# Transposes of activations by DMA instead of by TensorE, in an attention and FP4 FFN layer on eight cores

## The reference

```python
xn = layernorm(x)
q, k, v = xn @ WQ, xn @ WK, xn @ WV            # 16 heads of 64
attn = softmax(causal(q @ k.T / 8)) @ v @ WO
xq = fp4_quant_dequant(xn)                     # blocks of 16 along the last dim
h = silu(xq @ fp4(w_gate).T) * (xq @ fp4(w_up).T)      # 2816 wide
out = x + attn + fp4_quant_dequant(h) @ fp4(w_down).T
```

## Time and profile before

| | us |
|---|---|
| median of the runs | 8919.08 (8908.66 to 8929.5, 2 runs) |
| profiled execution, its own time | 8984.06 |
| its span, slowest core (core 5) | 8982.5 |
| spans of the eight cores | 8902.6 to 8982.5 |
| mean granted TensorE clock, dies 0 and 1 | 0.771 and 0.761 |

### The profile page before, as it was taken

The page is one execution under the profiler, slowest core; times in us unless marked ns, Lnnn a source line. Parts: engine busy times, 40 slices in busy tenths (PEclk is TensorE's granted clock), DMA queues, the critical chain, the costliest instruction groups (busy, mean ns, idle before and its releaser), DMA issues.

```text
span 8982.5 us, 81694 instructions; the slowest of 8 cores (8902.6 to 8982.5 us)
## 1 busy us (share of the span) xinstructions
PE 5393.8 (60%) x21392; PEld 2186.3 (24%) x21392; DVE 3172.4 (35%) x5268; ACT 2391.1 (27%) x4112; POOL 2267.7 (25%) x2237
## 2 busy tenths in 40 slices
PE   0000147665788457665778457666778367656877
PEld 0000013111333222111333222112333122112333
DVE  2444460001566540000666530001666530002665
ACT  0000133551111234550111234550111325541111
POOL 1434330110334221120333211110334211110443
PEclk9999968666888667666888676667888676667887
DMA  4222200002100100002110100002000100011000
GB/s 127 56 57 68 68 24 10 1 1 88 67 36 36 54 17 10 1 1 103 54 40 36 50 24 1 1 26 107 29 36 36 54 19 1 1 63 71 36 36 36
DMA packets 137330, 354.95 MB, mean 40 GB/s; under 512 B 76352, under 2 KB 77376, under 8 KB 132160
## 3 DMA queue, kind: packets, MB, share of 16 engines
q1 hardware_dynamic: 136896, 349.74, 11.2%
HBM read 255.85 MB, written 93.85 MB: 39 GB/s over the span
## 4 chain that ended last, share of the span: by engine, by line
PE 38%; DVE 25%; issue 10%; ACT 10%; DMA 8%; POOL 6%; DVEq 1%; SPq 1%; POOLq 0%; ACTq 0%
PE ps_c L610 10%; DVE heap L235 5%; ACT heap L597 4%; DVE heap L226 4%; POOL heap L604 4%; DVE heap L257 3%; PE ps_a L790 3%; PE ps_a L582 3%; DVE heap L229 3%; PE ps_a L548 3%; PE ps_b L548 3%; PE ps_c L697 3%; PE ps_a L732 2%; DVE heap L238 2%; DVE heap L810 2%
## 5 line engine op out<-in xcount | busy, mean ns | idle before, releaser
L245 POOL TENSOR_TENSOR heap<-heap 128x512 f32<-128x512 f32 (+3 forms) x564 | 914.0, 1621 | 3976.1 <-DVE heap L241 3976.1
L610 PE MATMUL ps_c<-heap 128*65 128x512 bf16 (+3 forms) x2560 | 1092.6, 463 | 766.7 <-POOL heap L604 372.6
L623 DVE CAST heap<-ps_c 64x512 bf16<-64x512 f32 x256 | 174.9, 683 | 2713.6 <-PE ps_c L610 2674.8
L604 POOL TENSOR_TENSOR heap<-heap,tri 128x128 bf16<-128x128 bf16 x1024 | 435.2, 425 | 2448.2 <-ACT heap L597 2336.9
L597 ACT ACTIVATE heap<-ps_a 128x512 bf16<-128x512 f32 (+1 forms) x1280 | 639.9, 551 | 728.0 <-PE ps_a L582 712.7
L247 POOL TENSOR_TENSOR heap<-heap 128x512 f32<-128x512 f32 (+3 forms) x564 | 764.5, 1355 | 81.7 <-POOL heap L245 1.3
L610 PEld LDWEIGHTS ps_c<-heap 128*65 128x65 bf16 x2560 | 312.9, 122 | 1654.3 <-issue 1641.7
L840 PE MATMUL ps_c<-heap 128*128 128x512 bf16 x2816 | 682.5, 407 | 5.0 <-ACT heap L874 5.0
L226 DVE TENSOR_REDUCE heap<-heap 128x32 f32<-128x512 f32 (+3 forms) x564 | 412.5, 731 | 504.4 <-DMA heap<-w_up 167.1
L597 ACT ACTIVATE heap<-ps_b 128x512 bf16<-128x512 f32 (+2 forms) x1280 | 590.6, 524 | 0.0
L235 DVE TENSOR_TENSOR heap<-heap 128x512 f32<-128x512 f32 (+3 forms) x564 | 501.2, 889 | 60.9 <-DVE heap L232 2.8
(11 more groups left out here) (78 smaller groups left out, 6302.7 us busy)
## 6 DMA issues: line engine op xcount, KB each, us to landing
heap<-x SPq DMA_DIRECT2D x128, 512.0 KB, 3.3
attn_scr<-heap SPq DMA_DIRECT2D x64, 512.0 KB, 2.6
heap<-attn_scr SPq DMA_DIRECT2D x64, 512.0 KB
out<-heap SPq DMA_DIRECT2D x64, 512.0 KB, 2.6
heap<-wg_d SPq DMA_DIRECT2D x4, 5632.0 KB, 19.8
heap<-wu_d SPq DMA_DIRECT2D x4, 5632.0 KB, 34.1
heap<-wd_d SPq DMA_DIRECT2D x4, 5632.0 KB
heap<-w_gate SPq DMA_DIRECT2D x22, 512.0 KB, 4.1
```

The lines of the kernel that those rows point to most:

```text
L245: P.emit("gpsimd", lambda e: e.tensor_tensor(u, u, M, op=ALU.add), waits=[(s_ve, ve_m), (s_po, s_po.n)], inc=(s_po, 1))
L604: P.emit("gpsimd", lambda e, eb=eb: e.tensor_tensor(eb[:, 0:128], eb[:, 0:128], tri[:], op=ALU.mult), waits=[(s_ac, ac_exp), (s_po, s_po.n ...
L610: pr=pr, s_=s_, vst=vst, jm=jmax: e.matmul(pv[:, off:off + n], vst[:, j, pr * 2 + s_, 0:65], eb[:, 0:n], start=(j == 0), stop=(j == jm - 1)),
```

## The change

The 128x128 transposes of xnb, xnq and hq are taken off TensorE, and their copies off ACT. In their place SP issues dma_start_transpose, one for each 128x128 block, from SBUF straight to the block's place in xnt, xnqt and hqt in SBUF. The weights' transposes in the first stage stay on TensorE. There are three new semaphores, s_trb, s_trq and s_trh, one for each kind. Who waited for TensorE's transpose (to overwrite xnb, xnq or hq) or for ACT's copy (to read xnt, xnqt or hqt) now waits for the DMA's semaphore. The transposes of xnq are no longer one tile late: they follow those of xnb in the same tile.

```diff
 # layer-norm stage, tile t
-                if t >= 1:
-                    pxnq, pt = pending_xnq
-                    for c in range(NCD):
-                        P.emit("tensor", lambda e, pxnq=pxnq, c=c: e.transpose(
...
                 for c in range(NCD):
-                    P.emit("tensor", lambda e, xnb=xnb, c=c: e.transpose(
-                        ps_t[:, c * 128:(c + 1) * 128], xnb[:, c * 128:(c + 1) * 128], idn[:]),
...
+                    P.emit("sync", lambda e, xnb=xnb, c=c, t=t, xnt=xnt: e.dma_start_transpose(
+                        xnt[:, c, t * 128:(t + 1) * 128], xnb[:, c * 128:(c + 1) * 128]),
+                        waits=([(s_ac, ac_xnb), (s_trb, s_trb.n)] if c == 0 else []),
+                        inc=(s_trb, 16))
+                tr_xnb_t = s_trb.n
+                xnb_rd = tr_xnb_t
+                for c in range(NCD):
+                    P.emit("sync", lambda e, xnq=xnq, c=c, t=t, xnqt=xnqt: e.dma_start_transpose(
+                        xnqt[:, c, t * 128:(t + 1) * 128], xnq[:, c * 128:(c + 1) * 128]),
+                        waits=([(s_ve, ve_xnq), (s_trq, s_trq.n)] if c == 0 else []),
+                        inc=(s_trq, 16))
+                xnq_rd[pp] = s_trq.n
+                ac_xnqt.append(s_trq.n)
 # V projection, then Q and K projection: what the first matmul waits for
-                            waits=([(s_ac, ac_xnt_t), (s_w, w_attn_ld)]
+                            waits=([(s_trb, tr_xnb_t), (s_w, w_attn_ld)]
...
-                                    waits=([(s_ac, max(evac_of_buf[bi], ac_xnqt[-1])),
+                                    waits=([(s_ac, evac_of_buf[bi]), (s_trq, ac_xnqt[-1]),
 # FFN stage: quant_deq into hq, and the down projection
-                                extra_pe_wait=tr_pe_done)
+                                extra=[(s_trh, tr_dma_done)])
...
-                                waits=([(s_ac, ac_tr_all), (s_sc2, w_d_ld)]
+                                waits=([(s_trh, tr_dma_done), (s_sc2, w_d_ld)]
 # FFN stage, end of tile t
-                    done = 0
-                    while done < NI:
-                        g = min(8, NI - done)
-                        for k in range(g):
-                            it = done + k
-                            P.emit("tensor", lambda e, it=it, k=k, hq=hq: e.transpose(
...
+                    for it in range(NI):
+                        P.emit("sync", lambda e, it=it, hq=hq, hqt=hqt: e.dma_start_transpose(
+                            hqt[:, it * 128:(it + 1) * 128], hq[:, it * 128:(it + 1) * 128]),
+                            waits=([(s_ve, ve_hq), (s_pe, s_pe.n), (s_trh, s_trh.n)]
+                                   if it == 0 else []),
+                            inc=(s_trh, 16))
+                    tr_dma_done = s_trh.n
```

More of the change, by code:

```diff
@@ L192, in build_core_program @@
         s_zg = [Sem(es, nc, "s_zg0"), Sem(es, nc, "s_zg1")]
+        s_trb = Sem(es, nc, "s_trb")
+        s_trq = Sem(es, nc, "s_trq")
+        s_trh = Sem(es, nc, "s_trh")
         s_st = Sem(es, nc, "s_st")
@@ L198, in build_core_program @@
         s_po = Sem(es, nc, "s_po")
-        ALL = (s_x, s_w, s_sc, s_sc2, s_zg[0], s_zg[1], s_st, s_ws, s_pe, s_ve, s_ac, s_po)
+        ALL = (s_x, s_w, s_sc, s_sc2, s_zg[0], s_zg[1], s_trb, s_trq, s_trh,
+               s_st, s_ws, s_pe, s_ve, s_ac, s_po)
         P = Prog()
@@ L249, in quant_pre, with quant_deq @@
             return (s_po.n, u_off, qs_off)
-        def quant_deq(tok, out_bf, F, extra_pe_wait=0):
+        def quant_deq(tok, out_bf, F, extra_pe_wait=0, extra=()):
             po_q, u_off, qs_off = tok
@@ L259, in quant_deq @@
                 u.rearrange("p (b w) -> p b w", w=16), scb, op=ALU.mult),
-                waits=[(s_po, po_q)] + ([(s_pe, extra_pe_wait)] if extra_pe_wait else []),
+                waits=[(s_po, po_q)] + ([(s_pe, extra_pe_wait)] if extra_pe_wait else [])
+                      + [w for w in extra if w[1]],
                 inc=(s_ve, 1))
@@ L460, in build_core_program @@
                     xnb, xt, AF.Identity, bias=nmb, scale=rstd),
-                    waits=[(s_pe, xnb_rd)], inc=(s_ac, 1))
+                    waits=[(s_trb, xnb_rd)], inc=(s_ac, 1))
                 ac_xnb = s_ac.n
@@ L467, in build_core_program @@
                 xnq = vb(L_XNQ[pp], D)
-                P.wait("vector", [(s_ac, ac_xn), (s_pe, xnq_rd[pp])])
+                P.wait("vector", [(s_ac, ac_xn), (s_trq, xnq_rd[pp])])
                 tok0 = quant_pre(xn[:, 0:512], L_U[0], L_M[0], L_QS[0], 512)
@@ L488, in build_core_program @@
-                pending_xnq = (xnq, t)
-                pending_ve = ve_xnq
-                for c in range(NCD):
-                    P.emit("tensor", lambda e, xnb=xnb, c=c: e.transpose(
-                        ps_t[:, c * 128:(c + 1) * 128], xnb[:, c * 128:(c + 1) * 128], idn[:]),
[L493 to L499, removed]
@@ L500, in build_core_program @@
-                ac_xnt_t = s_ac.n
+                for c in range(NCD):
+                    P.emit("sync", lambda e, xnb=xnb, c=c, t=t, xnt=xnt: e.dma_start_transpose(
[9 more added lines that the diff above has]
+                        inc=(s_trq, 16))
@@ L514, in build_core_program @@
                 ac_vevac = s_ac.n
[L515 to L527, removed]
             qt_sb = vb(QT, NP * S).rearrange("p (r q) -> p r q", q=S)
@@ L766, in build_core_program @@
             po_f_prev = 0
-            tr_pe_done = 0
-            ac_tr_all = 0
+            tr_dma_done = 0
             ve_f_prev = 0
@@ L824, in build_core_program @@
                     hbuf_rd[NICH - 1] = quant_deq(
-                        ptok, hq[:, pi0:pi0 + pilen], pilen, extra_pe_wait=tr_pe_done)
+                        ptok, hq[:, pi0:pi0 + pilen], pilen, extra=[(s_trh, tr_dma_done)])
                     ve_hq = s_ve.n
```

## The result

The changed kernel takes 10,475.92 us (median of 11 runs, 10,454.44 to 10,490.85), the kernel before 8,931.79 us beside it (10 runs). The ratio is 1.1714, 95% interval 1.1685 to 1.1744: slower by 1,544 us. The forecast was 10,600 us.

What follows compares the result with a forecast made beforehand. No engine bounds the whole, so stages were read singly; FFN 1408p - 774 plus layer norm 448p + 6 and 32p - 1 give 1888p - 769, +1685 at p = 1.3: 10,600 us, range 9,250 to 12,750.

Steps and rivals of the forecast that it cites:

- p: SP's queue, both stages: time one DMA transpose adds in a row of its kind, taken as 1.3 us between 0.52 and 3.1.
- 22p - 4 us: FFN: VectorE's wait, at the dequantising multiply that overwrites hq, for the transposes to land, 60 times.
- 8p + 3: Layer norm: wait of VectorE's L420 and the square for the x load queued behind xnq's eight transposes, in us.
- the third rival: FFN: TensorE cools in the stall and brings down late, 384 us, 10,980 at p = 1.3; chance inside the 0.65.
- 29.8 + 22p: FFN: new steady tile period, from 27.4 us of VectorE's chain, 0.34 issue, 2.0 landing and 22 transposes; 58.4 us at p = 1.3.
- 22p - 12.9: FFN: growth in us of each of 60 steady tiles, the new period against 42.7 before.
- 4 x 22p: FFN: extra for the last tile of each of four batches, where nothing covers the row of transposes.
- 18.7 + 8p: Layer norm: new tile period in us, against 18.6, with the x load queued behind eight transposes; 14 of 16 tiles.
- 448p + 32p + 5: Layer norm: whole growth, 448p + 6 for 56 tiles plus 32p - 1 for Q and K projections awaiting the last eight.
- The credit: FFN: TensorE starts the next tile's gate/up without awaiting transposes, VectorE starts at once; floor 34.0 us a tile against 42.7.
- The first: Both stages: a transpose costs no more than a plain issue, p = 0.34, -127 us, 8,790; chance 0.12 up to 0.5.
- The second: Both stages: each transpose finishes before the next, p up to 3.1, +5453, 14,370 us; chance 0.18 for p above 2.1.

Runs made afterwards that it cites:

- Experiment 4: The changed kernel with one DMA transpose instruction per row (192 instead of 2,432), same blocks and bytes: 8,579.71 us, ratio 0.956 to the kernel before.
- ffn_dma: The changed kernel with its layer-norm stage as before the change, so only the FFN's transposes go by DMA: 9,791.79 us, ratio 1.0901.
- ln_dma: The changed kernel with its FFN stage as before the change, so only layer norm's transposes go by DMA: 9,671.07 us, ratio 1.0762.
- experiment 9: The kernel before, hq's TensorE transposes emitted after gate and up of chunks 0 and 1 of the next tile: 8,423.42 us, ratio 0.9421.

## Why the prediction was right

The forecast of 10,600 us was 124 us above the measured 10,476. The mechanism was as told, in both stages; that the number is so near is in part luck, because p was a middle between far ends and because a term too dear in the FFN and terms too cheap in layer norm partly cancelled. Step by step:

*What is late next.* VectorE at the multiply into hq, 60 times: predicted 22p - 4 us, which is 23.9 at p = 1.27; measured 1330.0 / 60 = 22.2. VectorE at the sum over x: predicted 8p + 3 = 13.2 for 56 tiles; measured 13.7, 56 times. TensorE late with down (the third rival): its group after the stall is slow, 3.57 us for eight, yet down ends at 2719.0 and L826 starts at 2723.14, so it added nothing. The granted clock of the stage fell from 0.82 to 0.74, and still no steady tile ended on TensorE.

*The price p.* Taken as 1.3, measured 1.27. That was luck: no row had it, 0.52 and 3.1 were the ends, and the reason for the place between them was partly wrong. I leaned on the store in small pieces, as if the transfer of the pieces set the price. Experiment 4 shows that for single blocks it does not: the DMA engines were 0.17 busy, and eight times the data cost no more. The price is the instruction's. The Trainium skill's 1309 ns ("VectorE: DVE Perf Modes", The three transpose paths) lies 3% above the 1.27 us here; the traces add that an instruction of eight such blocks holds the queue no longer. The Trainium skill's "Advanced Engine Details and Errata" (X-Bar Transpose (TRN2)), by which these DMAs are as fast as regular ones, does not agree with what was measured. The changed kernel moves 44 GB/s in the row of hq. Even the wide instruction for it, 704 KB, lands 5.9 us after its issue (5.2 at least), where a plain 512 KB store takes 2.6.

*The FFN's sum.* At p = 1.27, 29.8 + 22p is 57.7 us a tile; the steady tile took 56.7. The row and its landing take 29.3 us and not 29.9, because the landing (2.3 us) runs from the last issue's start, and the 27.4 us were 26.8 in the tile shown. The larger error is in what this was compared with. The 42.7 us of the kernel before is the mean over 15 intervals, of which the last is no tile:

```profile
L849 DVE TENSOR_TENSOR heap<-ps_c,heap x15: 1223/1225/1225, 2357.4 to 2978.5; 128x1024 f32<-128x1024 f32 x15
...
2997.33 1.22 DVE L849 TENSOR_TENSOR heap<-ps_c,heap 128x1024 f32<-128x1024 f32 x1 [17.64 <-PE ps_c L840]
```

```profile
L826 DVE TENSOR_TENSOR heap<-ps_c,heap x15: 1224/1225/1225, 2553.9 to 3347.4; 128x1024 f32<-128x1024 f32 x15
...
3393.63 1.22 DVE L826 TENSOR_TENSOR heap<-ps_c,heap 128x1024 f32<-128x1024 f32 x1 [44.95 <-PE ps_c L817]
```

A steady tile took 621.1 / 14 = 44.4 us before and 793.5 / 14 = 56.7 after, so it lost 12.3 us and not 22p - 12.9 = 15.0; 1.7 of the missing 2.7 are the 42.7. The 4 x 22p for the last tiles was right: VectorE's wait there grew from 17.64 to 44.95 us, by 27.3, with 27.9 predicted. And the first row of a batch, which has no store ahead of it and was charged 15.0, cost 8. Together 14 x 12.3 + 27.3 + 8 = 208 us a batch, the stage's own growth, where 253 were predicted. Sum: predicted 1408 x 1.27 - 774 = +1,014, measured 4 x 208 = +832 by the stage's length and +800 in ffn_dma.

*Layer norm's sum.* Predicted 18.7 + 8p = 28.9 for a tile against 18.6, +10.3; the steady tile went from 18.4 to 29.8, +11.4, and 56 tiles were rightly counted. Half a microsecond of it is that x lands 3.7 us after its issue and not 3.2, with transposes before it on the queue (L411, against L406's 3.2 in the earlier trace rows):

```profile
DMA to landing us min/median/max: 3.4/3.7/15.9
```

The end of the stage, from the last tile to the Q and K projections, grew by 15 us a batch where 10 were charged. Predicted 448p + 32p + 5 = +615; measured +679 in ln_dma and 4 x 175 = +700 by the stage's length. In all, 1888 x 1.27 - 769 = 1,629 us were predicted at the measured p, and 1,544 came: about 180 too much in the FFN, 65 to 85 too little in layer norm.

*The credit.* That early gate and up let VectorE run on, 42.7 to 34.0 us if nothing else ended the tile, was right in size (34.3 in experiment 4; 44.4 to 35.2 for the steady tile) and, as experiment 9 shows, a matter of the order on TensorE alone.

*The rivals.* The first, a transpose as cheap as an issue, was wrong for the kernel as written and is close to what the wide kernel does: predicted 8,500 for VectorE as the bound, measured 8,580. The second, each waiting for the one before to land, is excluded: spacing 1.27, landing 2.3. The third did not happen: down ended 4 us early, with 5 predicted.

## What to carry to other kernels

Before moving work to a DMA queue, count instructions, not bytes: here one transpose instruction holds SP for 1.23 us whether it moves one 128x128 block or eight. 22 single ones in a row were 28 us that a single buffer (hq) put on VectorE's path, and an x load queued behind eight that wait for VectorE cost 11 us a tile. Whether a second buffer for hq would have hidden its row was not run. Write a row of transposes as one instruction, and put loads for later tiles ahead of anything on the queue that waits for compute. And when a stage gains from taking an operation off an engine, test whether the same operation, only later in that engine's order, gains as much: here it did. Last, before a mean over tiles goes into a sum, look at its first and last interval: here one of 15 hid 1.7 us of each tile.

## What was not expected of the hardware

- One DMA transpose of 128x1024 costs the same issue time as one of 128x128 (1.24 and 1.23 us). Behind a 512 KB store, 16 and 22 blocks take 3.15 and 4.0 us; with no store ahead, 1.8 to 2.0 and 3.3 to 3.7.
- A plain 512 KB load issued on the same queue behind eight transposes landed in 3.7 us and not in 3.2; it was hardly slowed.
- Behind 22 us in which it ran nothing, TensorE's first two groups took 3.57 and 1.89 us at a granted clock of 0.50 (1.2 GHz; 2701.93 to 2707.00), and the next took 1.05 at 0.99 (2.4 GHz). This slow start ended no tile.
